# Second layer's self attention: values on two column halves, row sums on GpSimd, one division a batch

## What is computed

```python
def _L1_attn_ref(x, W_qkv, b_qkv, W_out, b_out):     # x: 4 x 1024 x 256
    qkv = jnp.einsum('bse,ed->bsd', x, W_qkv) + b_qkv
    q, k, v = jnp.split(qkv, 3, axis=-1)              # width 64 each
    scores = jnp.einsum('bqh,bkh->bqk', q, k) * scale
    attn = jax.nn.softmax(scores, axis=-1)
    ctx = jnp.einsum('bqk,bkh->bqh', attn, v)
    return jnp.einsum('bqh,he->bqe', ctx, W_out) + b_out
...
x = _layernorm(x + _L1_attn_ref(x, L1_attn_W_qkv, L1_attn_b_qkv, L1_attn_W_out, L1_attn_b_out), axis=-1)
```

## Time and profile before

| | us |
|---|---|
| median of 3 executions | 2967.92 (2965.79 to 2970.15) |
| the profiled execution, its own time | 2970.13 |
| span of its profile | 2968.4 |
| the stage of the change | from 2333.7 to 2535 of the span |
| TensorE busy over the span | 2621.0 (88%) |
| VectorE, ScalarE, GpSimd busy | 1702.1, 1188.6, 1617.4 |

### The profile page before, as it was taken

One profiled execution on the slowest core, in us unless ns is written; L12 is line 12 of the kernel. 1 busy time (PEld: TensorE's weight loads), 2 busy tenths in 40 slices (PEclk: granted clock), 3 DMA queues, 4 the chain that ended last, 5 costly groups with the idle time before them and its releaser, 6 DMA issues. The chain is left out here.

```text
span 2968.4 us, 43608 instructions
## 1 busy us (share of the span) xinstructions
PE 2621.0 (88%) x12063; PEld 1627.1 (55%) x12063; DVE 1702.1 (57%) x3433; ACT 1188.6 (40%) x1674; POOL 1617.4 (54%) x1340
## 2 busy tenths in 40 slices
PE   7999999999999999999999968982696588798595
PEld 5666666666666666666666535542474244454254
DVE  5565665656656666665665635663234555568743
ACT  3444444444444444444444324551122334354334
POOL 2667766777766776677676752433333313333343
PEclk8999999999999999999999979996897599899698
DMA  6554465554555446455455311003894100000233
GB/s 174 114 129 111 103 131 110 121 122 99 118 118 128 109 103 134 108 124 119 99 122 118 80 55 36 2 2 114 318 351 136 46 0 1 30 2 9 60 115 91
DMA packets 406433, 301.60 MB, mean 102 GB/s; under 512 B 293495, under 2 KB 338463, under 8 KB 401343
## 3 DMA queue, kind: packets, MB, share of 16 engines
q1 hardware_dynamic: 390302, 230.78, 33.5%
q0 software_dynamic: 12080, 63.53, 6.1%
q10 hardware_dynamic: 3952, 6.08, 0.6%
HBM read 185.72 MB, written 94.13 MB: 94 GB/s over the span
## 5 line engine op out<-in xcount | busy, mean ns | idle before, releaser
L655 POOL TENSOR_TENSOR a_total<-a_total,a_pr 128x1024 f32<-128x1024 f32 x384 | 913.5, 2379 | 47.1 <-ACT a_pr L639 24.3
L639 ACT ACTIVATE a_pr<-a_psS 128x1024 f32<-128x1024 f32 x512 | 524.9, 1026 | 657.9 <-PE a_psS L627 657.9
L584 DVE TENSOR_REDUCE a_nmax<-a_psX 128x1 f32<-128x512 f32 x1024 | 694.0, 687 | 140.9 <-PE a_psX L579 138.1
L667 PE MATMUL a_psO<-a_pr,a_vd 128*64 128x512 f32 x2048 | 481.8, 602 | 0.0
L579 PE MATMUL a_psX<-a_kA,a_qA 128*128 128x512 f32 x1024 | 415.7, 408 | 17.4 <-issue 6.3
L655 POOL TENSOR_TENSOR a_total<-a_pr 128x1024 f32<-128x1024 f32 x64 | 153.2, 2394 | 488.7 <-ACT a_pr L639 488.7
L627 PE MATMUL a_psS<-a_qA,a_kA 128*128 128x512 f32 x1024 | 339.4, 413 | 2.5 <-DVE a_nT L600 1.4
L627 PE MATMUL a_psS<-a_qB,a_kB 128*128 128x512 f32 x1024 | 322.2, 396 | 0.1
L667 PEld LDWEIGHTS a_psO<-a_pr,a_vd 128*64 128x64 f32 x2048 | 129.9, 136 | 240.0 <-issue 188.2
L579 PEld LDWEIGHTS a_psX<-a_kA,a_qA 128*128 128x128 f32 x1024 | 194.0, 189 | 102.0 <-DVE a_nmax L584 23.5
L627 PEld LDWEIGHTS a_psS<-a_qA,a_kA 128*128 128x128 f32 x1024 | 181.4, 189 | 121.1 <-issue 90.1
(11 more groups left out here) (400 smaller groups left out, 4493.4 us busy)
## 6 DMA issues: line engine op xcount, KB each, us to landing
a_qA<-a_qhi SPq DMA_DIRECT2D x124, 256.0 KB
a_vd<-a_vg SPq DMA_DIRECT2D x128, 128.0 KB
a_kA<-a_khi SPq DMA_DIRECT2D x62, 256.0 KB
a_kA<-a_klo SPq DMA_DIRECT2D x62, 256.0 KB
a_kB<-a_khi SPq DMA_DIRECT2D x62, 256.0 KB
a_qB<-a_qlo SPq DMA_DIRECT2D x62, 256.0 KB
a_qhi<-a_ph SPq DMA_DIRECT2D x120, 128.0 KB, 3.4
a_qlo<-a_pl SPq DMA_DIRECT2D x120, 128.0 KB, 2.7
```

Source lines behind the costliest of these rows:

```text
L584: w.eng.tensor_reduce(nmax[:, half, u:u + 1], psX[:, half, :], AX.X, ALU.max, negate=True)\
L639: w.eng.activation(pr[:, n, :], psS[:, half, :, :].rearrange("p a b -> p (a b)"), ACT.Exp, scale=SCALE)\
L655: w.eng.tensor_tensor(total[:, buf, :], first, pr[:, n, :], ALU.add).then_inc(sems["ad"], 1)
L667: last = w.eng.matmul(psO[q * HD:(q + 1) * HD, :], vd[:, b, kc, :], pr[:, n, q * 512:(q + 1) * 512], start=kc == 0, stop=kc == KC - 1)
```

## The change

In the softmax of batch b each `values` call uses `vd` with 64 columns. The product for queries 0 to 511 goes to columns 0 to 63 of the array, that for queries 512 to 1023 to columns 64 to 127, into one bank of `psO`, which takes turns by batch. The row sums no longer come from ones in `vd`: POOL adds the 8 blocks of `pr` up into `total` with 7 additions of 128x1024 a batch. `pr` gets four buffers (RING), and an exponential waits for the addition that reads its buffer as well as for the product.

`divide` is split. `take_out`, at the old place, copies `psO` out by ACT in one instruction of 128x512. The new `divide` stands in batch b+1 behind `queries`: two products of `ones` with `total` into a bank of `psX`, then DVE turns, takes reciprocals and turns back (128x512, once), then POOL multiplies `oU` by `rec`. The output is kept as two halves of 512 queries on partitions 0 to 63 and 64 to 127, and `wo` is loaded twice, so that `outputs` takes its rows from either half. For the last batch `divide` is called after the loop, behind the four `add_bias` of that batch on POOL. One memset moves from POOL to a smaller one on DVE.

```diff
@@ buffers @@
-        wo = m.sb("wo", [HD, D])
+        wo = m.sb("wo", [P, D])
...
-        vd = m.sb("vd", [P, 2, KC, 2 * HD])
-        pr = m.sb("pr", [P, 2, S])
+        vd = m.sb("vd", [P, 2, KC, HD])
+        ones = m.sb("ones", [P, HD])
+        pr = m.sb("pr", [P, RING, S])
+        total = m.sb("total", [P, 2, S])
...
@@ scores @@
             if w.on("scalar"):
                 w.wait("s", w.at("s"))
-                w.wait("pv", w.at("s", 2))
-                w.eng.activation(pr[:, n, :], psS[:, n, :, :].rearrange("p a b -> p (a b)"), ACT.Exp, scale=SCALE)\
+                w.wait("pv", w.at("s", RING))
+                w.wait("ad", (KC - 1) * (b - 1) + KC - RING + kc if kc < RING else (KC - 1) * b + max(kc - RING, 1))
+                w.eng.activation(pr[:, r, :], psS[:, n, :, :].rearrange("p a b -> p (a b)"), ACT.Exp, scale=SCALE)\
                     .then_inc(sems["ex"], 1)
             w.inc("ex")
+            if kc:
+                if w.on("gpsimd"):
+                    w.wait("ex", w.at("ex"))
+                    if kc == 1:
+                        w.wait("rec", b - 1)
+                    else:
+                        w.wait("ad", w.at("ad"))
+                    w.eng.tensor_tensor(total[:, d, :], pr[:, 0, :] if kc == 1 else total[:, d, :], pr[:, r, :], ALU.add)\
+                        .then_inc(sems["ad"], 1)
+                w.inc("ad")
@@ values @@
                 for q in range(2):
-                    last = w.eng.matmul(psO[:, q, :], vd[:, d, kc, :], pr[:, n, q * 512:(q + 1) * 512],
+                    last = w.eng.matmul(psO[q * HD:(q + 1) * HD, d, :], vd[:, d, kc, :], pr[:, r, q * 512:(q + 1) * 512],
                                         start=kc == 0, stop=kc == KC - 1)
@@ divide @@
+        def take_out(w, b):
+
             if w.on("scalar"):
                 w.wait("pv", w.at("pv"))
-                w.wait("ot", w.at("ot", 1))
-                w.eng.activation(oU[:, cols], psO[:, h, :], ACT.Copy).then_inc(sems["nm"], 1)
+                w.wait("ot", w.at("ot"))
+                w.eng.activation(oU[:, :], psO[:, b % 2, :], ACT.Copy).then_inc(sems["nm"], 1)
             w.inc("nm")
...
+        def divide(w, b):
+
+
+            k = bank(w)
+            if w.on("tensor"):
+                if b == 0:
+                    w.wait("cstv", 4)
+                w.wait("ad", (KC - 1) * (b + 1))
+                w.wait(f"m{k}", w.at(f"m{k}"))
+                for q in range(2):
+                    last = w.eng.matmul(psX[q * HD:(q + 1) * HD, k, :], ones[:, :], total[:, b % 2, q * 512:(q + 1) * 512],
+                                        start=True, stop=True)
+                last.then_inc(sems["mi"], 1)
+            w.inc("mi")
+            if w.on("vector"):
+                w.wait("mi", w.at("mi"))
+                w.eng.transpose(turned[:, :], psX[:, k, :]).then_inc(sems[f"m{k}"], 1)
+                w.wait(f"m{k}", w.at(f"m{k}", -1))
+                w.link(w.eng.reciprocal(inv[:, :], turned[:, 0:512:32]), "dv")
+                w.wait("ot", w.at("ot"))
+                w.eng.transpose(rec[:, :], inv[:, :].unsqueeze(2).to_broadcast([P, 16, 32])).then_inc(sems["rec"], 1)
+            else:
+                w.inc("dv")
+            w.inc(f"m{k}")
+            w.inc("rec")
+            if w.on("gpsimd"):
                 w.wait("nm", w.at("nm"))
...
+                w.wait("rec", w.at("rec"))
+                w.eng.tensor_tensor(oT[:, b % 2, :], oU[:, :], rec[:, :], ALU.mult).then_inc(sems["ot"], 1)
@@ outputs @@
-                w.wait("ot", 2 * b + 1 + i // 2)
+                w.wait("ot", b + 1)
...
+                    half, c = i // 2, (2 * (i % 2) + tt) * P
+                    rows = slice(half * HD, (half + 1) * HD)
+                    last = w.eng.matmul(psX[:, k, tt * D:(tt + 1) * D], oT[rows, b % 2, c:c + P], wo[rows, :], start=True, stop=True)
@@ walk @@
                 if b + 1 < B:
                     queries(w, b + 1)
+                if b:
+                    divide(w, b - 1)
                 values(w, b, 0)
...
                 if b + 1 == B:
                     for i in range(OB):
                         add_bias(w, b, i)
-                for h in range(2):
-                    divide(w, b, h)
+                take_out(w, b)
+            divide(w, B - 1)
```

More of the change, by code:

```diff
@@ L2077, in layer1_self_attention @@
     OB = TB // 2
+    RING = 4
     with ExitStack() as ctx:
@@ L2094, in layer1_self_attention @@
         m16 = m.sb("m16", [P, 2 * KC], F32R)
[L2095 to L2099, removed]
+        oU = m.sb("oU", [P, 512])
+        turned = m.sb("turned", [P, 512])
+        inv = m.sb("inv", [P, 512 // 32])
+        rec = m.sb("rec", [P, 512])
+        oT = m.sb("oT", [P, 2, 512])
         xb = m.sb("xb", [P, OB, 2, D])
@@ L2202, in values_in @@
                 w.wait("mi", w.at("mi"))
-                w.eng.tensor_copy(vd[:, d, :, 0:HD], psX[:, k, :].rearrange("p (t d) -> p t d", d=HD)).then_inc(sems[f"m{k}"], 1)
+                w.eng.tensor_copy(vd[:, d, :, :], psX[:, k, :].rearrange("p (t d) -> p t d", d=HD)).then_inc(sems[f"m{k}"], 1)
             w.inc(f"m{k}")
@@ L2256, in scores @@
         def scores(w, b, kc):
-            d, n = b % 2, kc % 2
+            d, n, r = b % 2, kc % 2, kc % RING
             if w.on("tensor"):
@@ L2312, in add_bias @@
                 if b == 0 and i == 0:
-                    w.wait("wo", 32)
+                    w.wait("wo", 48)
                 w.wait("var", (b - 1) * OB + i + 1)
@@ L2325, in outputs @@
                 if b == 0 and i == 0:
-                    w.wait("wo", 32)
-                w.wait("ot", 2 * b + 1 + i // 2)
+                    w.wait("wo", 48)
+                w.wait("ot", b + 1)
                 w.wait(f"m{k}", w.at(f"m{k}"))
                 for tt in range(2):
-                    c = (2 * i + tt) * P
-                    last = w.eng.matmul(psX[:, k, tt * D:(tt + 1) * D], oT[:, b % 2, c:c + P], wo[:, :], start=True, stop=True)
+                    half, c = i // 2, (2 * (i % 2) + tt) * P
+                    rows = slice(half * HD, (half + 1) * HD)
+                    last = w.eng.matmul(psX[:, k, tt * D:(tt + 1) * D], oT[rows, b % 2, c:c + P], wo[rows, :], start=True, stop=True)
                 last.then_inc(sems["mi"], 1)
@@ L2467, in _ @@
             eng.dma_start(bkv[:, :], bcol[HD:3 * HD, :], allow_slow_non_contiguous=True).then_inc(sems["wk"], 16)
-            eng.dma_start(wo[:, :], w_out).then_inc(sems["wo"], 16)
+            for k in range(2):
+                eng.dma_start(wo[k * HD:(k + 1) * HD, :], w_out).then_inc(sems["wo"], 16)
             eng.dma_start(bo[:, :], b_out.partition_broadcast(P)).then_inc(sems["wo"], 16)
@@ L2473, in _ @@
             make_identity(eng, ident, sems["cst"])
-            eng.memset(vd[:, :, :, HD:2 * HD], 1.0).then_inc(sems["vd"], 1)
             eng.memset(rowmask[:, :, :], 0.0).then_inc(sems["cst"], 1)
@@ L2492, in _ @@
             eng.memset(kB[HD:HD + 16, :, :].bitcast(F32), 1.0).then_inc(sems["cstv"], 1)
-            eng.wait_ge(sems["cstv"], 3)
+            eng.memset(ones[:, :], 1.0).then_inc(sems["cstv"], 1)
+            eng.wait_ge(sems["cstv"], 4)
             eng.wait_ge(sems["wq"], 48)
```

15 lines of the change are left out of this document (3 added, 12 removed).

## The result

| | before | after |
|---|---|---|
| median, 19 executions each | 2969.44 (2964.28 to 2974.03) | 2975.69 (2968.36 to 2986.95) |
| ratio | | 1.0021 (95%: 1.0011 to 1.0031) |
| profiled execution, span | 2968.4 | 2978.5 |
| first exponential to the last sum of the stage | 161.98 | 169.57 |

The forecast was 1.1 us less, with a range that ended at 2975. The change costs 6.2 us (3 to 9 by the interval). The last row counts from the exponential of block 0 of batch 0 (2368.09 before, 2369.44 after) to the last sum on VectorE (2530.07, 2539.01): 7.6 us of the profile's 10.1 lie there.

The account below looks back on a forecast made before the run. TensorE was taken as the bound, values its largest user at 62.7 us. Terms -2.95 (batch 0), -2.4 and -2.4 (batches 1 and 2) and +6.6 (batch 3) sum to -1.1 us: 2966.8 against the median 2967.92, range 2961 to 2975.

Parts of the forecast that it names:

- Values on halves, 0.5 a call, and 0.35 for the change of form: TensorE's values product: column halves save 0.86 us a call, less 0.35 for going to halves and back, so 0.5.
- The variant with the change of form at nothing: Alternative sum with no cost for going to column halves and back: total -4.9 us, so 2963.0.
- Batch 0, -2.95: Batch 0: values 1 saves 0.15 us, values 2 to 6 save 2.5, values 7 gives 0.3; sum 2.95.
- values 7 lies beside the 1.22 us: End of a batch: values 7 outlasts VectorE's 1.22 us of writing `qB`'s extra rows by 0.3 us, which is gained.
- Batches 1 and 2, start: Shifted bank order makes the first keys product wait for `qB`, about 1.7 us; early savings buy nothing, 0.25 lost.
- Batches 1 and 2, -2.4 each: Savings of 2.68 us from values 2 to 6, less 0.35 for VectorE, plus 0.3, less 0.25 at the start.
- "No cost" under GpSimd: Batches 0 to 2: GpSimd's additions and multiplication, 29.4 of about 42 us busy, delay statistics but cost TensorE nothing.
- Batch 3, +6.6: Batch 3 with its end: GpSimd's queue sets the pace, last sum at 44.8 us instead of 38.16, costing 6.6 more.
- The clock: Slower rival: thinner TensorE work halves the clock in batches 1 and 2, up to 5 us each, 2977; chance 0.15.
- It decides from about 14 us more at 1.2 GHz: Threshold for the halved clock to decide the result: about 14 us more at 1.2 GHz than now, 7 us lost.
- scores to scores 2 to 3 us shorter: Sign of being right: scores to scores in batches 1 and 2 (2405.09 to 2447.68 now) 2 to 3 us shorter.
- the granted clock of 2405 to 2490 fell below 0.9: Sign of being wrong: TensorE's granted clock over 2405 to 2490 falls below 0.9.

## Why the prediction was wrong

By its own steps:

- **Values on halves, 0.5 a call, and 0.35 for the change of form.** Right: 0.51 and 0.36 measured. The 0.68 behind an outputs call wasn't measured by itself. The variant with the change of form at nothing comes to about 2962 by the same savings for each call, not 2963.0; no step here rests on it.
- **Batch 0, -2.95.** Measured -1.96, and -1.90 in the pair with added products. What failed is the end of the batch: "values 7 lies beside the 1.22 us ...; it now outlasts them by 0.3, and that is gained". The profile of before already had scores 0.05 us after the 1.22 (2402.63 + 1.22, scores at 2403.90). So values 7 hid nothing that could be gained, values 6 saves next to nothing ahead of VectorE's last maxima, and `s_m` is longer, held by a bias sum. TensorE waits 2.04 us for it instead of 1.40.
- **Batches 1 and 2, start.** Right: the wait, its cause and its length (1.62), and that the old division's end buys nothing.
- **Batches 1 and 2, -2.4 each.** At full clock it is -1.1 (-1.13 and -1.06). To block 7's exponential -1.35 was measured, and the forecast's terms give 1.6 to there (0.5, 0.68, 0.5, 0.5, less 0.35 and 0.25). From there, values 6 and 7 were to save 0.8, and the end of the batch got 0.25 longer. Of these 1.05, `s_m` is 0.56. The rest is the 0.3 of values 7, which wasn't there, and values 6, eaten by VectorE's lateness. This lateness is what "No cost" under GpSimd overlooked: its queue holds bias sums too, and that reaches TensorE by way of `psX`, whose banks the output sums free. The late bias sum is also the one that holds `s_m`. The prediction looked only at the path by ACT.
- **Batch 3, +6.6.** Measured +5.2, in all five profiles with this order of batch 3 (43.13 to 43.18 us). The mechanism and the order of the chain were right. The sum was 1.4 too large: the last addition ended 0.8 earlier, and the four bias sums took 4.93 for 5.38.
- **The clock.** This step decided it. The prediction had the mechanism, its signs and even the place, priced it at up to 5 us a batch and gave it 0.15, because batch 1 had held 1.00 and the first layer runs at full speed. Neither was evidence for thinner work: batch 1 of before is 88% busy on TensorE, and batch 2 of that same profile had already fallen once. The sum has nothing for it. The measured loss is 2.7 to 11.0 us in a batch, which made the batch 2.0 to 8.3 us longer, and both profiles of the unedited changed kernel lost over 10 us in these two batches. "It decides from about 14 us more at 1.2 GHz" was right in size: after lost 9.5 us more in the two batches than before, that is 19 us more at 1.2 GHz, and came out 6 us slower.

So two steps failed: the clock, put at nothing in the sum, and the end of batches 0 to 2, where GpSimd's later bias sums were put at no cost. Structure -1.1 forecast, +1.1 measured with the clock held in batches 1 and 2, and about 5 us of clock on top (6.2 less 1.1). That batch 3 came out 1.4 better than forecast hides part of what the other batches missed, 3.7 us; that was luck. Of the signs named, "scores to scores 2 to 3 us shorter" failed (1.0 longer), and the granted clock of 2405 to 2490 fell below 0.9, as the sign for the clock rival said.

## What to carry to other kernels

Count what a removed matrix product leaves behind on TensorE: where the engine already waits often and its clock has been seen to fall once nearby, less work is a risk of a few us a batch, and the price belongs in the forecast, not in a small rival. To tell it from a structural loss, put products that nobody reads into the waits of both kernels: the kernel that gets faster with more work was paying for the clock. And before work goes to an idle engine, look at what stands in its queue between two steps of a ring (statistics, bias sum, output sum), and move out of the ring what needn't be in it. Look also at what the longer queue pushes beside small instructions of VectorE: a bias sum that slipped some 4 us towards one (start to start 4.4 us before, 0.6 after, in batch 1) held it until it ended.

## What the hardware showed that I hadn't expected

- A GpSimd bias sum of 128x512 (1.26 us) holds VectorE's 128x8 tensor_scalar until it ends: 0.70 to 0.84 us instead of 0.17, ending 0.02 to 0.04 us behind it in 18 of 18 cases. With bias sums back to back the next one holds the 128x8 scalar_tensor_tensor behind it as well, 1.18 instead of 0.17. VectorE's addition holds GpSimd's 128x2 instruction in the same way, 1.02 instead of 0.20.
- An fp32 addition of 128x1024 takes 2.38 us on GpSimd and 1.19 on VectorE.
- In the 90 us of batches 1 and 2 the mean granted clock was 0.85 to 0.94 in all six profiles of the changed kernel that add on GpSimd and have no added products, and 1.00 in all four that have them, for 12 to 18 products of 0.43 us in these two batches that nobody reads. The kernel that makes its row sums by TensorE holds 1.00 too.
